# Centring and splitting the last stage's gate and up weights in the grouped attention instead of in the last stage

## The chip, the cores and the metric

The kernel runs on one core of a Trainium2 chip. The metric is the device time of one execution in microseconds (us); the median of three runs is compared. A measurement of this kernel tells a difference of about 0.3%, some 3 us, from none.

## The reference

The program is a network of four layers on 2048 rows (8 sequences of 256) of width 128 in float32. Each layer is an attention and a feed-forward part, each of the form x = x + layernorm(part(layernorm(x))). The two parts between which the change moves work are these:

```python
# layer 2: grouped attention (16 query heads, 4 groups), then an FFN with one of 8 experts for each sequence
raw = einsum('bsgwe,btge->bstgw', Q, K / 8);  attn = softmax(raw, axis=2)
A = einsum('bstgw,btge->bsgwe', attn, V);     attention = X + A @ Wpost
logits = gelu(last_token @ Wp1 + bp1) @ Wp2 + bp2;  sel = argmax(softmax(logits))
h = gelu(hidden @ W1[sel] + b1[sel]);         ffn = hidden + 0.3 * ((h @ W2[sel] + b2[sel]) @ Wo + bo)
# layer 3 (the last stage): attention over channels, then a mixture of 8 experts, H = 342
z = softmax(einsum('byq,byk->bkq', q, k) / sqrt(128));  attention = merge(einsum('byz,bvy->bvz', z, v)) @ Wo.T
w, sel = top_k(distance(x, centroid), 2);  w = softmax(w)
for e in range(8):
    h = silu(xs @ Wg[e] + bg[e]) * (xs @ W1[e] + b1[e])
    out = out + we[:, e:e+1] * (h @ W2[e] + b2[e])
```

## The kernel before

The rows stay in SBUF for the whole run, and the stages follow each other: attention and experts of layer 0, attention and FFN of layer 1, grouped attention with its FFN (layer 2, some 540 to 842 us), and the last stage (layer 3, 843 us to the end). Each engine has an instruction stream of its own; semaphores order them.

**Split weights.** A float32 product is made from three matmuls of rounded parts. For the last stage, the gate and up weights of an expert are a tile of 128 x 684 (128 rows of the hidden width, 2 x 342 columns). They have to be centred (less their last row, spread over all partitions: the tile `last_row`), then rounded (`gu_hi`), and what the rounding left is the low part (`gu_lo`). The matmuls of the experts read `gu_hi`, `gu_lo` and `down`.

**Who does it before.** At the end of the grouped attention SyncE loads the raw weights of all 8 experts into `gu_lo` ("gu", L1525), the plane of last rows ("plane", L1527) and the down weights ("down", L1530). In the last stage VectorE subtracts the last row (`less_last`, L2244 to L2247), ScalarE copies with rounding (`high`, L2430 to L2432), and VectorE subtracts the rounded part (`split`, L2249 to L2252): 24 operations for 8 experts. `mixed_events` (L1986) lists the order of the last stage's first part by hand: for each of the 4 runs of 512 rows the channel attention (`c_stats`, `c_norm`, `c_proj`, `c_scores`, `c_zn`, `c_shift`, `c_res`), the router (`stats`, `norm`, `score`), and the sending of rows to the experts' blocks by GpSimd (`send`, L1712). VectorE, ScalarE and TensorE run through the same list. The tables `less`, `highs` and `splits` say behind which event each of the 24 operations stands. TensorE waits for all splits (`split_ready`, L2691) ahead of the first expert block.

**The grouped attention.** `grouped_attention_ffn` (L2717) runs a pipeline of steps s = 0 to 12, each with 8 sub-steps u, over 8 sequences: in step s, sequence s - 2 is turned and its row maxima are taken, sequence s - 3 is scored, s - 4 is scaled, s - 5 is normed and added to x. GpSimd adds two halves of the probabilities once for each u (`key_halves`, L2897) and does a few small operations (input and output reciprocal roots, L2907, and the residual). SyncE's loop runs over s = 2 to 12 and has only DMAs: `place(s - 3, 1)`, then `spread(s - 4)`, then `place(s - 2, 0)` (L2819, L2831). `place` brings row maxima into the operand `maxima`, which TensorE needs for the scores (L3369); `spread` sends reciprocals out to DRAM and back. Each waits for semaphores, and SyncE handles them strictly one after another. Behind the loop SyncE waits for the last transposed scores, and then `ffn.load_experts(0)` (L348) loads the experts that the first sequences have chosen: six DMAs, for which it reads the choices (`choose`, VectorE, L397). "gu" follows, then the experts of the other sequences, "plane" and "down". The FFN's `first` matmul (L524) waits for the experts.

Of the kernel before, what the change touches and what calls it, by code (L numbers as in the profile page):

```python
# [9 lines left out]
F32 = mybir.dt.float32  # L10
# [1503 lines left out]
def load_experts(eng, layer, src_gu, src_down, w, plane=None, parts=("gu", "plane", "down")):  # L1514
# [9 lines left out]
    if "gu" in parts:  # L1524
        eng.dma_start(w["gu_lo"][:, :, :].bitcast(F32), src_gu[0:n, :, :].rearrange("e p f -> p e f")).then_inc(w["loaded"], 16)  # L1525
    if plane is not None and "plane" in parts:
        eng.dma_start(w["last_row"][:, :, :], plane.rearrange("p (e f) -> p e f", e=n)).then_inc(w["loaded"], 16)  # L1527
# [6 lines left out]
def expert_weights(nc, ctx, layer):  # L1534
# [10 lines left out]
    else:  # L1545
        w["last_row"] = sb("last_row", [P, n, width], F32)
# [439 lines left out]
def mixed_events(W):  # L1986
# [3 lines left out]
    less = {("c_stats", 0): [0], ("c_stats", 1): [1], ("c_norm", 1): [2], ("c_scores", 0): [3], ("c_stats", 2): [4],  # L1990
            ("stats", 0): [5], ("norm", 1): [6], ("stats", 2): [7]}
    highs = {("c_norm", 0): [0, 1], ("c_zn", 0): [2, 3], ("norm", 0): [4, 5], ("norm", 1): [6], ("norm", 2): [7]}
    splits = {("c_norm", 1): [0, 1], ("c_shift", 0): [2, 3], ("c_shift", 1): [4], ("c_shift", 2): [5], ("norm", 2): [6],
              ("c_shift", 3): [7]}

    def with_weights(e):
        return ([e] + [("high", s) for s in highs.get(e, [])] + [("split", s) for s in splits.get(e, [])]
                + [("less_last", s) for s in less.get(e, [])])

    events = with_weights(("c_stats", 0)) + with_weights(("c_norm", 0))  # L2000
    for k in range(RUNS + 3):
# [6 lines left out]
        for e in step:  # L2008
            if 0 <= e[1] < RUNS and e[0] in ("ranked", "routed"):
                events += ranked if (e[0] == "ranked") == (d == RUNS // 2) else []  # L2010
            elif 0 <= e[1] < RUNS and (e[0] != "early" or d == RUNS // 2):
                events += with_weights(e)
# [7 lines left out]
def experts(nc, g, layer, key, w, mix=None, out=None, route=None, load_next=None):  # L2020
# [17 lines left out]
    with ExitStack() as ctx:  # L2038
# [37 lines left out]
        hi_ready, split_ready = st.sem("hi_ready"), st.sem("split_ready")  # L2076
# [11 lines left out]
        if by_distance:  # L2088
            c2_ready, c2_ps, less_ready, stored = (st.sem(n) for n in ("c2_ready", "c2_ps", "less_ready", "stored"))
# [55 lines left out]
        def _(sp):  # L2145
            if not by_distance:
                load_next(sp)
# [68 lines left out]
        def _(dve):  # L2216
# [26 lines left out]

            def less_last(e):  # L2244
                dve.wait_ge(w["loaded"], w["parts"])
                raw_gu = raw_gate_up(w, layer, e)
# [1581 lines left out]
```

## Time and profile before

| | |
|---|---|
| median of three runs | 1046.18 us (1043.87 to 1046.47) |
| profiled execution, its time | 1044.56 us |
| profiled execution, its span | 1042.8 us |
| TensorE (PE) busy | 929.9 us, 89% of the span |
| VectorE (DVE) busy | 685.3 us, 66% |
| ScalarE (ACT) busy | 518.3 us, 50% |
| GpSimd (POOL) busy | 462.1 us, 44% |

A profile is one execution; busy time counts instructions at work, not waits. The views used below are: stretches (busy time of each engine, TensorE's granted clock, share of the DMA engines), groups by line (mean duration of one instruction, and idle time before them), waits (an engine's instruction, what released it, us in all, times, longest), a single tile's or line's instructions, the page's list of DMA issues, and the timeline (start, duration, line, and in brackets the idle time before with its releaser). SPq is SyncE issuing DMAs. In names, `a_` is the attention's tile, `m_` the mixture's, `e_` an expert weight.

### The profile page before, as it was taken

The numbers are of one execution on the slowest core, as the hardware profiler recorded it, in microseconds if no ns is written. First come the engines' busy times: TensorE is split into PE (matmuls) and PEld (weight loads), VectorE is DVE, ScalarE is ACT, GpSimd is POOL, SyncE is SP. The second block draws the span as 40 slices with busy tenths as digits, with TensorE's granted clock in tenths as the row PEclk, the third lists the DMA queues.
The fourth block names the chain that finished last, engine by engine and source line by source line (L and its number), as shares of the span: only waits on it lengthen the run. The fifth ranks groups of instructions, "written<-read, shape, count | busy, mean of one in ns | idle before, by whom it ended". The sixth has DMA issues, their size and how long they took to land. (4 is left out here: it accounts for less than half of the span.)

```text
span 1042.8 us, 23846 instructions
## 1 busy us (share of the span) xinstructions
PE 929.9 (89%) x8240; PEld 730.2 (70%) x8240; DVE 685.3 (66%) x1910; ACT 518.3 (50%) x1023; POOL 462.1 (44%) x512
## 2 busy tenths in 40 slices
PE   7998989799993899999989999999999977869990
PEld 6666667698993766565776676776766866869990
DVE  4687874565445778888487658676577777764444
ACT  2566654244443378786545545444445434324442
POOL 2355554555445313232463334333456432685443
PEclk9999998999997999999999999999999988989996
DMA  8421100222213024222210011110121820022214
GB/s 276 110 74 56 60 2 2 70 68 68 59 42 87 12 74 140 64 64 66 71 32 2 5 40 43 43 42 3 42 43 42 275 77 1 27 67 72 58 47 121
DMA packets 80750, 66.42 MB, mean 64 GB/s; under 512 B 6706, under 2 KB 73441, under 8 KB 80251
## 3 DMA queue, kind: packets, MB, share of 16 engines
q1 hardware_dynamic: 71899, 54.34, 18.9%
q0 software_dynamic: 4512, 8.47, 2.4%
q10 hardware_dynamic: 4224, 2.10, 0.8%
q8 instruction: 70, 1.15, 0.5%
q14 instruction: 45, 0.37, 0.1%
HBM read 38.76 MB, written 26.58 MB: 63 GB/s over the span
## 5 line engine op out<-in xcount | busy, mean ns | idle before, releaser
L832 DVE TENSOR_REDUCE a_rowmax<-a_banks 128x4 f32<-128x1024 f32 (+1 forms) x112 | 136.8, 1221 | 46.6 <-PE a_banks L1245 19.0
L2897 POOL TENSOR_TENSOR a_both<-a_probs 128x512 f32<-128x512 f32 x64 | 85.7, 1340 | 138.7 <-ACT a_probs L3205 138.6
L1057 ACT ACTIVATE a_probs<-a_banks 128x1024 f32<-128x1024 f32 x112 | 114.8, 1025 | 64.7 <-PE a_banks L1231 48.7
L2182 POOL DMA_INDIRECT acc<-m_result,m_yb x77 | 75.7, 983 | 80.1 <-DVE m_result L2319 40.2
L3205 ACT ACTIVATE a_probs<-a_banks 128x1024 f32<-128x1024 f32 x64 | 65.6, 1025 | 89.7 <-PE a_banks L3376 89.7
L2451 ACT ACTIVATE m_gate<-m_banks 128x352 f32<-128x352 f32 (+1 forms) x93 | 42.8, 460 | 97.8 <-PE m_banks L2612 97.7
L3055 DVE TENSOR_REDUCE a_rowmax<-a_banks 128x4 f32<-128x1024 f32 x64 | 77.8, 1219 | 10.2 <-PE a_banks L3349 10.2
L1712 POOL DMA_INDIRECT rows<-m_yrow,m_idx x64 | 64.8, 1012 | 30.6 <-issue 19.3
L700 POOL TENSOR_SCALAR_AFFINE_SELECT a_probs<-a_probs 128x512 f32<-128x512 f32 (+1 forms) x48 | 37.9, 789 | 76.7 <-ACT a_probs L1057 76.7
L3392 PE MATMUL a_banks<-a_probs,a_V 128*64 128x256 f32 x512 | 69.4, 392 | 0.0
L2304 DVE TENSOR_TENSOR m_h<-m_banks,m_gate 128x342 f32<-128x342 f32 (+1 forms) x55 | 28.5, 517 | 55.5 <-ACT m_gate L2451 43.6
L2638 PE MATMUL m_banks<-e_down,m_hT 128*128 (+2 forms) x462 | 64.9, 277 | 0.0
L1195 PE MATMUL a_banks<-ident 128*128 128x128 f32 x374 | 54.3, 292 | 7.7 <-DMA w_att<-in_att 6.1
L2638 PEld LDWEIGHTS m_banks<-e_down,m_hT 128*128 128x128 f32 (+2 forms) x462 | 58.3, 193 | 0.2 <-issue 0.2
L1273 PE MATMUL a_banks<-a_probs,a_V 128*32 128x256 f32 x720 | 58.0, 394 | 0.0
L2610 PE MATMUL m_banks<-e_gu_hi,m_y_hi 128*128 x154 | 56.3, 366 | 0.4 <-issue 0.4
L1195 PEld LDWEIGHTS a_banks<-ident 128*128 128x128 f32 x374 | 48.3, 202 | 11.1 <-DMA w_att<-in_att 6.1
L1231 PE MATMUL a_banks<-a_QT,a_KT 25*128 25x256 f32 x384 | 48.4, 327 | 6.5 <-DVE a_rowmax L832 4.2
L2611 PE MATMUL m_banks<-e_gu_lo,m_y_hi 128*128 x154 | 49.7, 322 | 0.0
L2612 PE MATMUL m_banks<-e_gu_hi,m_y_lo 128*128 x154 | 49.6, 322 | 0.0
L2301 DVE SCALAR_TENSOR_TENSOR m_h<-m_banks,m_yb,m_gate 128x352 f32<-128x352 f32 x38 | 22.2, 583 | 40.9 <-ACT m_gate L2451 40.9
L1245 PE MATMUL a_banks<-a_KT,a_QT 24*128 24x256 f32 x384 | 48.2, 329 | 0.9 <-ACT a_KT L1069 0.9
(420 smaller groups left out, 2552.2 us busy)
## 6 DMA issues: line engine op xcount, KB each, us to landing
rows<-fill SPq DMA_DIRECT2D x16, 520.0 KB, 4.4
a_factor<-recip_rows SPq DMA_DIRECT2D x28, 256.0 KB, 4.7
rows<-fill SPq DMA_DIRECT2D x15, 455.0 KB, 4.2
m_yb<-rows SPq DMA_DIRECT2D x77, 65.0 KB
a_expert<-in_experts SPq DMA_DIRECT2D x16, 257.5 KB, 2.9
e_gu_lo<-in_gu SPq DMA_DIRECT2D x1, 2736.0 KB
e_last_row<-in_last_rows SPq DMA_DIRECT2D x1, 2736.0 KB
e_gu_lo<-in_gu SPq DMA_DIRECT2D x1, 2464.0 KB, 10.2
```

The source lines that it names most:

```text
L832: nc.vector.reduce_max(o, src, AX).then_inc(rowmax_ready, 1)
L1057: nc.scalar.activation(probs[h][:, k, :, :], ps[:, 4:6, :], ACT.Exp, scale=SCALE).then_inc(exp_done, 1)
L1195: mm(ps[:, bank, 0:P], g.ident[:, :], g.ident[:, :], start=True, stop=True)
L1273: last = mm(o[:, 0:SEQ], v, probs[h][:, b // 2 + (0 if causal else 2 * kt), jj, (b % 2) * SEQ:(b % 2 + 1) * SEQ], start=kt == 0, stop=kt = ...
L1712: self.nc.gpsimd.indirect_dma_start(self.rows.rearrange("n p c -> (n p) c"), bass.IndirectOffsetOnAxis(self.idx[:, c:c + 1], 0), self.yrow ...
L2182: nc.gpsimd.indirect_dma_start(acc.rearrange("k n d -> (k n) d"), bass.IndirectOffsetOnAxis(yb[b % YB][:, P:P + 1].bitcast(U32), 0), resul ...
L2610: mm(o, y_hi[i % 3][:, :], gu_hi[:, s], start=True, stop=False)
L2638: last = mm(ps[:, out_bank(i), 0:P], hT[i % 2][0:r, c, :], part[0:r, c, :], start=c == 0, stop=c == FC - 1)
L2897: nc.gpsimd.tensor_tensor(both[u % 4][:, :, :], p[:, :, 0, :], p[:, :, 1, :], ALU.add).then_inc(both_ready, 1)
L3055: nc.vector.reduce_max(rowmax[i % 2][:, :, j, :, n].rearrange("p t h -> p h t"), ps[:, b:b + 2, :].rearrange("p h (t k) -> p h t k", t=T), ...
L3205: nc.scalar.activation(probs[u % 4][:, :, :, :].rearrange("p h t q -> p h (t q)"), ps[:, 4:6, :], ACT.Exp, scale=SCALE).then_inc(exp_done, 1)
L3392: last = mm(ps[h * D64:(h + 1) * D64, 6, 0:SEQ], V[i % 3][:, kt, j, :], probs[b][:, h, kt, :], start=kt == 0, stop=kt == T - 1)
```

## The change

In steps s = 4 to 11 of the grouped attention, expert e = s - 4 is centred, rounded and split. SyncE loads its raw weights into a new tile `centred` and its last-row plane into a new tile `rounded` (`load_raw`, one step ahead). GpSimd subtracts at u = 0, ScalarE copies with rounding at u = 1, GpSimd subtracts at u = 3. SyncE stores both parts to DRAM scratch (`store_split`). Both SyncE parts stand in the loop between `spread` and `place(s - 2, 0)`. There is one pair of tiles, so `load_raw(e + 1)` waits for the stores of e. Behind the loop "lo" is loaded in the place of "gu", after a wait for all stores; "plane" is gone, and "hi" is loaded at the start of the last stage. The 24 operations of the last stage, their semaphores and their three tables are gone, and TensorE waits for the loads where it waited for the splits.

```diff
--- before.py
+++ after.py
@@ -1521,10 +1521,11 @@
         for c in range(FC):
             r = P if c < FC - 1 else last_rows
             eng.dma_start(w["last_down"][0:r, c, :], src_down[n, c * P:c * P + r, :]).then_inc(w["loaded"], 16)
-    if "gu" in parts:
+    if n < NE:
         eng.dma_start(w["gu_lo"][:, :, :].bitcast(F32), src_gu[0:n, :, :].rearrange("e p f -> p e f")).then_inc(w["loaded"], 16)
-    if plane is not None and "plane" in parts:
-        eng.dma_start(w["last_row"][:, :, :], plane.rearrange("p (e f) -> p e f", e=n)).then_inc(w["loaded"], 16)
+    for k in ("lo", "hi"):
+        if split is not None and k in parts:
+            eng.dma_start(w[f"gu_{k}"][:, :, :].bitcast(F32), split[k].rearrange("e p f -> p e f")).then_inc(w["loaded"], 16)
...
@@ -1543,7 +1544,7 @@
         w |= {"last_gu_hi": sb("last_gu_hi", [P, width]), "last_gu_lo": sb("last_gu_lo", [P, width]),
               "last_down": sb("last_down", [P, FC, P], F32), "raw_gu": sb("raw_gu", [P, width], F32)}
     else:
-        w["last_row"] = sb("last_row", [P, n, width], F32)
...
@@ -1987,17 +1988,7 @@
 
 
 
-    less = {("c_stats", 0): [0], ("c_stats", 1): [1], ("c_norm", 1): [2], ("c_scores", 0): [3], ("c_stats", 2): [4],
-            ("stats", 0): [5], ("norm", 1): [6], ("stats", 2): [7]}
-    highs = {("c_norm", 0): [0, 1], ("c_zn", 0): [2, 3], ("norm", 0): [4, 5], ("norm", 1): [6], ("norm", 2): [7]}
-    splits = {("c_norm", 1): [0, 1], ("c_shift", 0): [2, 3], ("c_shift", 1): [4], ("c_shift", 2): [5], ("norm", 2): [6],
-              ("c_shift", 3): [7]}
-
-    def with_weights(e):
-        return ([e] + [("high", s) for s in highs.get(e, [])] + [("split", s) for s in splits.get(e, [])]
-                + [("less_last", s) for s in less.get(e, [])])
-
-    events = with_weights(("c_stats", 0)) + with_weights(("c_norm", 0))
+    events = [("c_stats", 0), ("c_norm", 0)]
     for k in range(RUNS + 3):
         a, b, c, d = k, k - 1, k - 2, k - 3
         step = [("c_shift", c), ("c_res", c), ("c_scores", b), ("c_proj", a), ("stats", c), ("send", d - 1, 3),
@@ -2009,7 +2000,7 @@
             if 0 <= e[1] < RUNS and e[0] in ("ranked", "routed"):
                 events += ranked if (e[0] == "ranked") == (d == RUNS // 2) else []
             elif 0 <= e[1] < RUNS and (e[0] != "early" or d == RUNS // 2):
-                events += with_weights(e)
+                events.append(e)
...
@@ -2143,7 +2133,9 @@
 
         @block.sync
         def _(sp):
-            if not by_distance:
+            if by_distance:
+                load_first(sp)
+            else:
                 load_next(sp)
...
-
-            def less_last(e):
-                dve.wait_ge(w["loaded"], w["parts"])
-                raw_gu = raw_gate_up(w, layer, e)
-                nc.vector.tensor_tensor(raw_gu, raw_gu, w["last_row"][:, e, :], ALU.subtract).then_inc(less_ready, 1)
-
-            def split(e):
-                dve.wait_ge(hi_ready, e + 1)
-                gu_hi, gu_lo, _ = weights(e)
-                nc.vector.tensor_tensor(gu_lo, raw_gate_up(w, layer, e), gu_hi.bitcast(F32), ALU.subtract).then_inc(split_ready, 1)
...
 
         @block.scalar
         def _(act):
-            def high(e):
-                act.wait_ge(less_ready, e + 1)
-                nc.scalar.activation(weights(e)[0], raw_gate_up(w, layer, e), ACT.Copy).then_inc(hi_ready, 1)
...
                 if kind == "slot":
@@ -2688,7 +2660,7 @@
                         pe.wait_ge(route.spot_ready, RUNS)
                     if r == first_early - 1:
                         if by_distance:
-                            pe.wait_ge(split_ready, NE)
+                            pe.wait_ge(w["loaded"], w["parts"])
...
@@ -2755,6 +2727,9 @@
         recip = st.sb("recip", [P, SEQ])
         factor = st.sb("factor", [P, NG, 2, SEQ])
         head_rows = st.sb("head_rows", [P, PAIRS, P])
+        width = 2 * F_EXP[3]
+        centred = st.sb("centred", [P, width], F32R)
+        rounded = st.sb("rounded", [P, width], F32R)
...
@@ -2840,20 +2817,37 @@
                     sp.dma_start(factor[D64 * h:D64 * h + D64, :, n, :],
                                  recip_rows[i % 2, k:k + 1, :, :].to_broadcast([D64, NG, SEQ])).then_inc(factor_ready, 16)
 
+            def load_raw(e):
+                if not 0 <= e < NE:
+                    return
+                if e >= 1:
+                    sp.wait_ge(split_stored, 32 * e)
+                sp.dma_start(centred[:, :].bitcast(F32), raw_gu[e, :, :]).then_inc(raw_loaded, 16)
+                sp.dma_start(rounded[:, :].bitcast(F32), raw_last[:, e * width:(e + 1) * width]).then_inc(raw_loaded, 16)
+
+            def store_split(e):
+                if not 0 <= e < NE:
+                    return
+                sp.wait_ge(low_ready, e + 1)
+                sp.dma_start(split["lo"][e, :, :], centred[:, :].bitcast(F32)).then_inc(split_stored, 16)
+                sp.dma_start(split["hi"][e, :, :], rounded[:, :].bitcast(F32)).then_inc(split_stored, 16)
+
             sp.dma_start(head_rows[:, :, :], head_rows_dram).then_inc(head_rows_loaded, 16)
             for s in range(2, SLOTS):
                 if s - 3 in valid:
                     place(s - 3, 1)
                 if s - 4 in valid and s - 4 != LAST:
                     spread(s - 4)
+                store_split(s - 4)
+                load_raw(s - 3)
                 if s - 2 in valid:
                     place(s - 2, 0)
             sp.wait_ge(sT_ps, S * SEQS)
             ffn.load_experts(sp, 0, experts_dram)
-            last_loads(sp, "gu")
+            sp.wait_ge(split_stored, 32 * NE)
+            last_loads(sp, "lo")
             ffn.load_experts(sp, 1, experts_dram)
             ffn.load_experts(sp, 2, experts_dram)
-            last_loads(sp, "plane")
             last_loads(sp, "down")
 
...
 
+            def less_last(e):
+                pool.wait_ge(raw_loaded, 32 * (e + 1))
+                nc.gpsimd.tensor_tensor(centred[:, :].bitcast(F32), centred[:, :].bitcast(F32), rounded[:, :].bitcast(F32),
+                                        ALU.subtract).then_inc(less_ready, 1)
+
+            def low_part(e):
+                pool.wait_ge(rounded_ready, e + 1)
+                nc.gpsimd.tensor_tensor(centred[:, :], centred[:, :].bitcast(F32), rounded[:, :].bitcast(F32),
+                                        ALU.subtract).then_inc(low_ready, 1)
+
             def key_halves(i, u):
 
                 n = S * i + u
@@ -2900,6 +2904,10 @@
                 i0, i4 = s, s - 5
                 if s - 3 in valid:
                     key_halves(s - 3, u)
+                if u == 0 and 0 <= s - 4 < NE:
+                    less_last(s - 4)
+                if u == 3 and 0 <= s - 4 < NE:
+                    low_part(s - 4)
                 if u == 1 and i0 in valid:
                     in_power(i0)
                 if u == 2 and i4 in valid:
@@ -3276,6 +3284,9 @@
                 i, v = (i2, u - 1) if u else (i2 - 1, S - 1)
                 if i in valid:
                     to_sbuf(i, v)
+                if u == 1 and 0 <= s - 4 < NE:
+                    act.wait_ge(less_ready, s - 3)
+                    nc.scalar.activation(rounded[:, :], centred[:, :].bitcast(F32), ACT.Copy).then_inc(rounded_ready, 1)
...
 
+        split = {k: nc.dram_tensor(f"split_{k}", [NE, P, 2 * F_EXP[3]], F32).ap() for k in ("lo", "hi")}
+
         def load_last(sp, part):
-            load_experts(sp, 3, a["gu3"], a["down3"], w3, a["last_rows"], [part])
-
-        grouped_attention_ffn(nc, g, "att2", a["head_rows"], w3, load_last, "ffn2", a["experts2"])
-        experts(nc, g, 3, "moe3", w3, mix="att3", out=out_dram)
+            load_experts(sp, 3, a["gu3"], a["down3"], w3, split, [part])
+
+        grouped_attention_ffn(nc, g, "att2", a["head_rows"], w3, load_last, "ffn2", a["experts2"], a["gu3"], a["last_rows"], split)
+        experts(nc, g, 3, "moe3", w3, mix="att3", out=out_dram, load_first=lambda sp: load_last(sp, "hi"))
 
```

## Rows read from the trace of the kernel before

**Rows 1.** By stretch: us, busy (count) per engine, TensorE clock, DMA share, GB/s.

```profile
674.00:706.00 32.00, 32.00 (x304) 22.71 (x304) 23.00 (x35) 15.46 (x24) 12.32 (x11) 1.00 0.16 35
...
800.00:843.00 43.00, 38.90 (x262) 33.60 (x260) 32.56 (x127) 16.00 (x36) 22.63 (x31) 1.00 0.64 210
...
843.00:880.00 37.00, 29.87 (x149) 24.91 (x150) 27.97 (x126) 16.36 (x34) 9.31 (x12) 0.82 0.02 5
...
916.00:918.00 2.00, 1.99 (x18) 1.99 (x19) 1.40 (x9) 0.21 (x1) 1.64 (x2) 0.55 0.10 33
```

**Rows 2.** By line, VectorE, 843 to 935 us: busy us, mean ns, idle.

```profile
L2247 DVE TENSOR_TENSOR e_gu_lo<-e_gu_lo,e_last_row 128x684 f32<-128x684 f32 x8 | 6.9, 864 | 1.4 <-DMA e_down<-in_down 1.4
...
L2252 DVE TENSOR_TENSOR e_gu_lo<-e_gu_lo,e_gu_hi 128x684 fp32r<-128x684 f32 x8 | 6.7, 862 | 0.0
```

**Rows 3.** Waits, 843 to 935 us: who, for whom, us, times, longest.

```profile
DVE x L2382 <- ACT m_cf L2438: 3.6, 4, 0.9
...
DVE m_yrow L1757 <- POOL m_in_rstd L1692: 3.5, 3, 1.7
```

**Rows 4.** A tile's and a line's instructions: ns least/median/most, first and last start.

```profile
L2432 ACT ACTIVATE e_gu_hi<-e_gu_lo x8: 760/764/772, 848.1 to 905.8; 128x684 fp32r<-128x684 f32 x8
...
L708 POOL TENSOR_TENSOR e_gu_lo<-e_gu_lo,e_gu_hi x14: 920/924/930, 57.8 to 173.2; 128x352 fp32r<-128x352 f32 x14
...
L1525 SPq DMA_DIRECT2D e_gu_lo<-in_gu x2: 426/430/435, 11.3 to 813.7; - x2
...
L2897 POOL TENSOR_TENSOR a_both<-a_probs x64: 1262/1278/1692, 558.1 to 801.0; 128x512 f32<-128x512 f32 x64
```

**Rows 5.** Page, part 6: DMA issues, KB each, median us to landing.

```profile
a_factor<-recip_rows SPq DMA_DIRECT2D x28, 256.0 KB, 4.7
...
a_expert<-in_experts SPq DMA_DIRECT2D x16, 257.5 KB, 2.9
```

**Rows 6.** Timeline, four engines, 806 to 815 us: start us, us, line, idle before.

```profile
806.20 0.15 DVE L397 FIND_INDEX8 a_chosen<-a_best,a_logits 6x8 uint32<-6x8 f32 x1
...
807.37 6.32 SPq L348 DMA_DIRECT2D a_expert<-in_experts  x6
...
812.57 0.71 POOL L2907 TENSOR_TENSOR a_out_rstd<-a_out_var,minus_half 128x2 f32<-128x2 f32 x1 [5.42 <-DVE a_out_var L2963]
...
814.33 1.89 PE L524 MATMUL a_banks<-a_yT_f,a_expert 128*128 128x256 f32 x8
```

**Rows 7.** Timeline, TensorE, 906 to 921 us, around an idle time.

```profile
906.69 5.60 PE L2533 MATMUL m_banks<-ident 128*128 128x128 f32 x48
...
916.01 0.20 PE L1960 MATMUL m_banks<-m_one_hot,m_upper 128*128 128x64 bf16 x1 [3.72 <-DVE m_chosen L1818]
...
916.31 4.49 PE L2533 MATMUL m_banks<-ident 128*128 128x128 f32 x24
```

**Rows 8.** Timeline, steps 7 to 8 and 9 to 10, two engines.

```profile
700.95 1.35 POOL L2897 TENSOR_TENSOR a_both<-a_probs 128x512 f32<-128x512 f32 x1 [2.00 <-ACT a_probs L3205]
...
715.93 0.43 PE L3369 MATMUL a_banks<-a_maxima,a_ones_row 64*128 64x512 f32 x2
...
763.52 1.29 POOL L2897 TENSOR_TENSOR a_both<-a_probs 128x512 f32<-128x512 f32 x1 [1.00 <-ACT a_probs L3205]
...
774.88 0.50 PE L3369 MATMUL a_banks<-a_maxima,a_ones_row 64*128 64x512 f32 x2 [0.20 <-ACT a_probs L3205]
```

**Rows 9.** Timeline, VectorE and GpSimd, 868 to 931 us.

```profile
868.87 1.56 POOL L1692 TENSOR_TENSOR m_in_rstd<-m_in_var,minus_half 128x4 f32<-128x4 f32 x1 [6.07 <-DVE m_in_var L1750]
...
884.57 1.04 POOL L1692 TENSOR_TENSOR m_in_rstd<-m_in_var,minus_half 128x4 f32<-128x4 f32 x1 [3.69 <-DVE m_in_var L1750]
...
893.71 0.86 DVE L2252 TENSOR_TENSOR e_gu_lo<-e_gu_lo,e_gu_hi 128x684 fp32r<-128x684 f32 x1
...
893.79 1.70 POOL L1712 DMA_INDIRECT rows<-m_yrow,m_idx  x1 [0.19 <-issue]
...
930.20 0.96 POOL L1712 DMA_INDIRECT rows<-m_yrow,m_idx  x1 [0.30 <-issue]
```

More of the change, by code:

```diff
@@ L1511, with load_experts @@
 ROWS_DOWN = {0: F_EXP[0], 3: F_EXP[3] + 1}
-def load_experts(eng, layer, src_gu, src_down, w, plane=None, parts=("gu", "plane", "down")):
+def load_experts(eng, layer, src_gu, src_down, w, split=None, parts=("down",)):
     n = ROUTED[layer]
@@ L1545, in expert_weights @@
     else:
-        w["last_row"] = sb("last_row", [P, n, width], F32)
+        sb("scratch", [P, n, width], F32)
     w["offset"], w["bytes"], w["gu_hi_bytes"] = offset, nc.sbuf_base - offset, 4 * n * width
@@ L2017, in mixed_events, with experts @@
     return events + [("map", 0)] + [("slot", s) for s in range(W + 2)]
-def experts(nc, g, layer, key, w, mix=None, out=None, route=None, load_next=None):
+def experts(nc, g, layer, key, w, mix=None, out=None, route=None, load_next=None, load_first=None):
     width = F_EXP[layer]
@@ L2088, in experts @@
         if by_distance:
-            c2_ready, c2_ps, less_ready, stored = (st.sem(n) for n in ("c2_ready", "c2_ps", "less_ready", "stored"))
+            c2_ready, c2_ps, stored = (st.sem(n) for n in ("c2_ready", "c2_ps", "stored"))
             (c_in_var, c_in_rstd, c_y_ready, c_yT_ps, c_yT_ready, c_qk_ps, c_qk_ready, c_v_ps, c_v_ready, c_z_ps,
@@ L2398, in _ @@
                     route.share(dve, r)
-                if kind == "less_last":
-                    less_last(r)
-                if kind == "split":
-                    split(r)
                 if kind == "early":
@@ L2496, in _ @@
                     route.ratio(act, r)
-                if kind == "high":
-                    high(r)
                 if kind == "gap" and r == RUNS - 1 and by_distance:
@@ L2714, with grouped_attention_ffn @@
 GQA = [("wq", NH * D64), ("wk", NG * P), ("wv", NG * D64), ("wpost", NH * D64)]
-def grouped_attention_ffn(nc, g, key, head_rows_dram, w, last_loads, ffn_key, experts_dram):
+def grouped_attention_ffn(nc, g, key, head_rows_dram, w, last_loads, ffn_key, experts_dram, raw_gu, raw_last, split):
     SCALE = float(D64) ** -0.5
@@ L2773, in grouped_attention_ffn @@
         q_raw, k_raw = st.sem("q_raw"), st.sem("k_raw")
+        raw_loaded, less_ready, rounded_ready, low_ready, split_stored = (
+            st.sem(n) for n in ("raw_loaded", "less_ready", "rounded_ready", "low_ready", "split_stored"))
         both_ready, head_rows_loaded, factor_ps = (st.sem(n) for n in ("both_ready", "head_rows_loaded", "factor_ps"))
```

1 line of the change is left out of this document (removed).

## The prediction

> **What bounds the kernel now.** I read the view of stretches first [rows 1]. In a steady step of the grouped attention (674 to 706 us) TensorE is busy for all of its 32.00 us at full clock, while VectorE has 23.00, ScalarE 15.46 and GpSimd 12.32: work put on the last two there has cover. Between 800 and 843 us, where the selected feed-forward (FFN) runs, TensorE is again nearly full (38.90 of 43). In the first part of the last stage, 843 to 880 us, nobody is: TensorE 29.87 of 37 at a mean clock of 0.82, VectorE 27.97. That is a chain that goes round the engines, and an instruction costs there only what no other engine's delay covers.
>
> So I read next what the change takes out [rows 2]: eight subtractions in L2247, 864 ns each, and eight in L2252, 862 ns: 13.8 us of VectorE. The waits say what stood behind them [rows 3]: four times VectorE reached the residual L2382 and still waited for ScalarE, 3.6 us in all, and three times it waited for GpSimd before L1757, 3.5 us in all. Most of the 13.8 us were put into such gaps.
>
> **The change part by part.**
>
> New work in the attention. A 128x684 subtraction on GpSimd has no row; the nearest are 128x352 at 0.924 and 128x512 at 1.278 us [rows 4], which is 2.2 ns for a column, so I take 1.66 us. Sixteen are 26.5 us on GpSimd, two in each of steps s = 4 to 11, and eight copies of 0.764 us [rows 4] on ScalarE. The first of a step (less_last, u = 0) stands behind the key halves of u = 0, the second (low_part, u = 3) behind those of u = 3. For the steady steps I charge 0: GpSimd is free for over 19 us of a step. Without that cover the pair would cost 3.3 us a step.
>
> The wait on SyncE. store_split stands in the SP loop and waits for low_part. In step s = 11 that is low_part(7), and on GpSimd it is behind the reciprocal root of step 11, u = 2 (L2907), which waits for the attention's sequence 6 and runs at 812.57 for 0.71 us [rows 6]. So low_part(7) ends at 812.57 + 0.71 + 1.66 = 814.9. What is queued behind SyncE's wait are the FFN's six expert loads. They were chosen when L397 ended (806.20 + 0.15 = 806.35), and the first was issued 1.02 us later, at 807.37 [rows 6]. Now SyncE issues two stores at 814.9 (0.43 us each [rows 4] and a small gap, 0.95 in all) and then needs the same 1.02: the first expert load is issued at 816.9. From issue to landing the median is 2.9 us for an expert [rows 5], so it lands at 819.8 at the earliest. It shares the DMA engines with the two stores of 342 KB; the slowest similar row, 4.7 us [rows 5], gives 821.6. I take 820.3, nearer to the expert's own row. TensorE began the first expert's matmuls at 814.33, with no idle time before them [rows 6]. So it starts **6.0 us** later (5.5 to 7.3). Nothing else is queued on TensorE there, and the FFN after it is TensorE's own stretch [rows 1], so the delay goes to the end. The load of "lo" behind the experts moves too, by about 9 us; its need is over 100 us away.
>
> The clock after that gap. After an idle time of 3.72 us (until 916.01) the granted clock was 0.55 in 916 to 918 [rows 1, 7], that is mostly at the lower of the two levels, 1.2 GHz. 24 filler matmuls took 4.49 us there, where 48 of the same kind took 5.60 before [rows 7]: a loss of 4.49 - 2.80 = 1.7 us. The new gap is longer. I take **2 us** (0 to 3.3: nothing if the loads set the pace in those microseconds anyway, twice the row's if the low level lasts twice as long).
>
> The step from s = 9 to s = 10. SyncE's place(7, 0) puts row maxima where the scores of u = 0 of step 10 read them. TensorE used them at 774.88 [rows 8]. Now store_split(5) and load_raw(6) stand before it. low_part(5) follows the key halves of 763.52 + 1.29 = 764.8 [rows 8] and ends at 766.5; two stores are issued by 767.4; their landing has no row, and I bound it by 2.9 and 4.7 us [rows 5]: 770.3 to 772.1; two raw loads are issued in 0.95; then the first two place transfers, about 0.6 us each, and their own landing, for which I have no row but the 2.9 us of an expert [rows 5]: 775.4 to 777.2 in all. The stall is 0.5 to 2.3 us, 0 if so small a transfer lands sooner, 3 if the raw loads hold it up. I take **1.5 us**. In a steady step the key halves of u = 3 start at 700.95 and the next step's scores at 715.93 [rows 8]: 15.0 us, where step 9 has 11.4. The same sum leaves 1.3 to 3.1 us to spare there: 0, bounded at 1 for each of five steps.
>
> The last stage. Taken out are the sixteen VectorE and eight ScalarE operations, and the wait for all weights ahead of the first. Gone through one after the other along the timeline, I find these gains. First, the wait for the weights falls away, at most its 1.4 us idle [rows 2]; but TensorE, which was at 0.82 of its clock in 843 to 880 [rows 1], bounds the steps behind it, and I take 0.4. Second, GpSimd's root L1692 takes 1.56 us when a removed subtraction runs beside it, 1.04 when none does [rows 9]: 0.5 us, and VectorE waits for that one. Third, from 890 to 922 us GpSimd's row sends bound the chain, and a send that meets a removed subtraction (893.71) takes 1.70 us instead of 0.96 [rows 9]; two more are alike (1.59 at 898.83, 1.69 at 911.03). Three times about 0.7 are 2.1, of which the filler matmuls ahead of the ranks let perhaps 1.2 through. The other thirteen subtractions lie under the waits of rows 3 or under TensorE, and come to 0. Sum: a gain of **2 us** (0.4 if only the first counts; 5 if half-clock stretches vanish as well). The cover is ScalarE's cf and GpSimd's sends; they are late next.
>
> On the third gain the Trainium skill's page "SBUF — State Buffer", section "Who interferes with whom", says otherwise: a VectorE tensor_tensor takes only the read interface that it shares with GpSimd and should not hold up descriptor generation. The rows differ (1.70 beside one, 0.96 without), so I go by them. By that page the gain would be about 0.9 instead of 2.
>
> TensorE's new wait for the weights costs 0: "hi" is issued as the last stage begins, and the first block's matmuls come over 80 us later.
>
> Sum: 6.0 + 2 + 1.5 - 2 = +7.5 us. The profiled execution took 1044.56 us, 1042.8 of it span; so that would be 1052.1. The median of the three runs is 1.6 higher, 1046.18; against it the forecast is **1053.7 us**.
>
> **The rivals.**
>
> Faster. VectorE is the engine that bounds the last stage and the freed time is worth its length: the sixteen subtractions give 13.8 us, the attention and FFN cost 9.5: -4.3, 1041.9. For it speaks that VectorE is busy for three quarters of 843 to 880. Against it speak the waits of rows 3 and that fillers and GpSimd's sends set most of the steps. It decides from a gain above 12.6 us in the last stage.
>
> No change. The expert loads don't come late, because the hold on SyncE is shorter than I read or something else of the FFN hides it: 1.5 - 2 = -0.5, 1045.7. Only the order of the code speaks against it, but strictly: one queue, one wait.
>
> Slower still. Every one of the steps 4 to 9 stalls for its row maxima, not the last alone: five more at about 1.5 us, 1061. For it speaks that SyncE's new chain of store, landing, load is some 8 us long in each step; against it the 1.3 to 3.1 us to spare.
>
> **How the numbers follow.** A measurement of this kernel tells 0.3% from no change, 3.1 us. The forecast's mechanism has 0.72, and its own range is 1048 to 1060: all low ends (5.5 + 0 + 0 - 5) would give 1046.7, all high ones (7.3 + 3.3 + 3 - 0.4) 1059.4. Slower still has 0.07, no change 0.13, faster 0.08. The low end of the forecast reaches below 1049.3, which I count as 0.03. So slower by over 0.3% is 0.76, within it 0.16, faster 0.08. For eight in ten the range has to reach into no change or into slower still: 1046.5 to 1060.
>
> **What would show it.** In the profile after, the six expert loads are issued at about 817 to 823, not 807; TensorE idles some 6 us before the first expert's matmuls, with a low clock behind it; SyncE's wait before is for GpSimd's low_part. GpSimd's subtraction is near 1.66 us. The scores of s = 10 wait for the transfer of row maxima. In the last stage the sends at 890 to 922 are all near 1 us, and the first block comes 2 us sooner after the stage's begin. I would be wrong if the expert loads are issued before 812, or if the last stage is shorter by more than 5 us.

## The result and the profile after

Over 20 runs of each kernel the median went from 1044.21 to 1048.86 us. The ratio is 1.0037 with a 95% interval of 1.002 to 1.0054: 3.9 us slower (2.1 to 5.6), where +7.5 was forecast; the two medians alone are 4.7 us apart, inside that interval. The sign and the place were right; the size came out at about half.

The profiled execution of the changed kernel took 1046.88 us. The first lines of its page, the span and the busy time of each engine:

```profile
span 1045.2 us, 23878 instructions
...
PE 923.8 (88%) x8240; PEld 725.4 (69%) x8240; DVE 675.2 (65%) x1894; ACT 518.1 (50%) x1023; POOL 483.7 (46%) x528
```

VectorE lost 10 us of busy time and GpSimd gained 22; TensorE was busy for 6 us less and yet the span is 2.4 longer. The stretches that answer to [rows 1]:

```profile
674.00:706.00 32.00, 32.00 (x302) 22.46 (x300) 22.30 (x35) 16.49 (x26) 15.97 (x13) 1.00 0.28 76
...
800.00:843.00 43.00, 35.86 (x225) 31.27 (x218) 28.16 (x118) 14.89 (x33) 20.75 (x27) 0.96 0.52 164
843.00:880.00 37.00, 28.95 (x161) 23.38 (x159) 20.07 (x102) 11.60 (x25) 9.03 (x15) 0.86 0.22 77
```

A steady step of the attention still has TensorE full for 32.00 us, with GpSimd at 15.97 instead of 12.32: the two subtractions are hidden there, as predicted. In 800 to 843 us TensorE lost 3 us and some clock. SyncE's timeline shows why, and GpSimd's the instruction it waited for:

```profile
812.24 0.33 SPq L2832 DMA_DIRECT2D split_lo<-a_centred  x1
812.61 0.43 SPq L2833 DMA_DIRECT2D split_hi<-a_rounded  x1
814.49 5.90 SPq L348 DMA_DIRECT2D a_expert<-in_experts  x6
820.43 0.43 SPq L1528 DMA_DIRECT2D e_gu_lo<-split_lo  x1
```

```profile
809.90 0.71 POOL L2915 TENSOR_TENSOR a_out_rstd<-a_out_var,minus_half 128x2 f32<-128x2 f32 x1 [5.44 <-DVE a_out_var L2971]
810.59 1.63 POOL L2891 TENSOR_TENSOR a_centred<-a_centred,a_rounded 128x684 fp32r<-128x684 f32 x1
```

The choice of experts was ready at 803.53 + 0.15 = 803.7 here. The loads could have been issued 1 us after that, at 804.7. They were issued at 814.49, behind the last low part (it ends at 812.22) and its two stores. TensorE's timeline, with the idle time and its releaser in brackets:

```profile
806.30 5.52 PE L3517 MATMUL a_banks<-late_w_att,a_craw 128*128 128x128 f32 x48
817.74 3.34 PE L524 MATMUL a_banks<-a_yT_f,a_expert 128*128 128x256 f32 x8 [5.92 <-DMA a_expert<-in_experts]
```

The first expert's matmuls waited 5.92 us for their weights and then took 3.34 us where [rows 6] has 1.89.

**Two single profiles have to be laid on a common event.** The attention's first matmul stands at 538.62 us before and at 532.71 after, though nothing ahead of it was changed: 5.9 us of chance. From there to the end the changed kernel took 8.3 us longer (2.4 + 5.9). Of these, 1.5 lie ahead of the attention's first key halves (21.0 us after its first matmul, where the kernel before has 19.45). They aren't the change's: e2 and h1, which run the attention of the kernel before, have 21.15 there. The following table therefore counts from event to event, read from the timelines of all the profiles of this study, one profile for each kernel: (a) first to last key halves of the attention, against the kernel before; (b) last key halves to the first expert's matmul; (c) from there to the last stage's first matmul; (d) to its first expert block; (e) to the end.

| kernel | a | b | c | d | e |
|---|---|---|---|---|---|
| before | 0 | 13.4 | 30.1 | 86.0 | 112.4 |
| after | +1.7 | 19.5 | 31.2 | 84.0 | 112.3 |
| e1, last store behind the loads | +1.4 | 13.4 | 32.2 | 81.9 | 111.5 |
| e2, last stage alone | 0.0 | 13.4 | 30.1 | 82.0 | 112.2 |
| e3, attention alone | +1.3 | 19.3 | 31.6 | 87.3 | 113.7 |
| e4, store and place moved | +2.3 | 13.4 | 32.0 | 81.8 | 112.1 |
| f1, SyncE's order rewritten | +2.3 | 13.4 | 30.5 | 83.9 | 111.4 |
| f2, all a step or more earlier | +1.0 | 13.4 | 30.1 | 81.8 | 111.5 |
| g3, after with fillers in the gap | +1.0 | 19.9 | 30.2 | 83.8 | 111.9 |
| h1, before with fillers | +0.2 | 13.4 | 30.1 | 86.0 | 114.5 |
| g1, before with three small subtractions | +0.2 | 13.4 | 30.1 | 88.2 | 112.1 |
| g2, before with three one-input operations | +0.2 | 13.4 | 30.1 | 88.1 | 112.0 |

Some 1.4 us in column a of e4 and f1 come from a stretch at the lower clock in step 3 that the other kernels don't show; whether their order brings it about stays open.

### The profile page after: what moved, and what is told of

Read it like the earlier page. It is cut to its first block and busy times, and to the rows that moved or that the text cites. A ratio compares the mean times of both kernels' runs of the same rounds, so it can differ in the third digit from the quotient of the medians.

```text
span 1045.2 us, 23878 instructions
## 1 busy us (share of the span) xinstructions
PE 923.8 (88%) x8240; PEld 725.4 (69%) x8240; DVE 675.2 (65%) x1894; ACT 518.1 (50%) x1023; POOL 483.7 (46%) x528
## 3 DMA queue, kind: packets, MB, share of 16 engines
q8 instruction: 70, 1.15, 0.5%
## 5 line engine op out<-in xcount | busy, mean ns | idle before, releaser
L1713 POOL DMA_INDIRECT rows<-m_yrow,m_idx x64 | 62.2, 972 | 32.5 <-issue 19.9
L1195 PEld LDWEIGHTS a_banks<-ident 128*128 128x128 f32 x374 | 47.0, 198 | 12.4 <-DMA w_att<-in_att 6.7
L2595 PE MATMUL m_banks<-ident,m_h 128*128 128x128 f32 (+2 forms) x279 | 47.0, 277 | 2.1 <-issue 0.7
```

The lines of the kernel that those rows point to most:

```text
L1195: mm(ps[:, bank, 0:P], g.ident[:, :], g.ident[:, :], start=True, stop=True)
L1713: self.nc.gpsimd.indirect_dma_start(self.rows.rearrange("n p c -> (n p) c"), bass.IndirectOffsetOnAxis(self.idx[:, c:c + 1], 0), self.yrow ...
```

## Experiments

**e1: the last store behind the expert loads.** My theory A was the sum of the prediction; theory B, that the last stage gives back about 5 us and not 2.

```diff
-                store_split(s - 4)
+                if s - 4 != LAST:
+                    store_split(s - 4)
...
             ffn.load_experts(sp, 0, experts_dram)
+            store_split(LAST)
             sp.wait_ge(split_stored, 32 * NE)
```

> The changed kernel with one thing moved: SyncE stores the last expert's parts (e = 7) behind the first FFN expert loads, not ahead of them. Theory A (my sum: the late expert loads cost 6.1 us and the low clock behind them 1.5, the attention costs 1.7, the last stage gives back 2.2): the expert loads are issued about 1 us behind the choice, TensorE has no idle time before the first expert's matmuls, and the time is that of the kernel before -0.5 us (-2 to +1). Theory B (the last stage gives back about 5 us on average, and the two single profiles compared hide that): the same repair of the loads, and the kernel before -3.5 us. Theory C (the FFN makes up for late loads, and the changed kernel's cost lies in the attention): the kernel before +3 us, as in the changed kernel.

Measured: 0.9985 of the kernel before (0.9955 to 1.0014), 1.6 us faster with an interval from 4.7 faster to 1.5 slower, which holds A and B and leaves out C. Column b is back at 13.4 us, so one DMA pair in SyncE's queue made the whole delay. Column c is 2.2 us longer than before instead, which none of the theories had. SyncE and TensorE of this run:

```profile
819.48 0.33 SPq L2832 DMA_DIRECT2D split_lo<-a_centred  x1
...
824.04 0.37 SPq L1528 DMA_DIRECT2D e_gu_lo<-split_lo  x1
830.04 2.20 SPq L348 DMA_DIRECT2D a_expert<-in_experts  x2
```

```profile
836.06 1.10 PE L524 MATMUL a_banks<-a_yT_f,a_expert 128*128 128x256 f32 x4 [2.16 <-DMA a_expert<-in_experts]
```

The 2.7 MB of "lo", issued at 824.04, go ahead of the other sequences' experts, issued at 830.04, and TensorE waits 2.16 us for these. In the kernel before, the load of the same size was issued 0.6 us ahead of the first expert's matmul, here 5.2 us behind it. The Trainium skill's page "DMA: Bandwidth & Descriptors", section "Queues, rings and completion order", has each ring consumed in order on its DMA engine; these rows agree, and f1 below tests it.

**e2: the last stage's part alone.** The attention is that of the kernel before, the 24 operations are left out, and raw weights are loaded where the parts would be:

```diff
-        split = {k: nc.dram_tensor(f"split_{k}", ...).ap() for k in ("lo", "hi")}
+        split = {"lo": a["gu3"].rearrange("e p f -> p e f"), "hi": a["last_rows"].rearrange("p (e f) -> p e f", e=NE)}
```

> The last stage's part of the change alone: the grouped attention is that of the kernel before, the 24 operations of the last stage are left out, and raw weights of the same size are loaded where the finished parts would be (so centring and splitting are left out of the computation). Theory A: the kernel before -2.2 us (-1 to -3.5). Theory B: the kernel before -5 us. If VectorE bound the last stage: -10 us or more.

Measured: 0.995 (0.992 to 0.998), 5.2 us faster (2.1 to 8.4): nearest to theory B, though the interval's end touches the 2.2 of theory A (f2 below decides). Laid on the kernel before at the last stage's first matmul, the first block comes 4.0 us sooner, and the timelines show where. 0.27 us: the wait for the weights (2.0 us gained at first, of which TensorE's own chain takes back the rest). 0.55: the root of [rows 9] takes 1.01 us instead of 1.56. 1.15: a stretch at the lower clock is gone (below). What is left, 2.07, goes nearly all to three sends, together 1.88 us shorter. Two of them on GpSimd's timeline; the first answers to the send of 1.70 us in [rows 9], the second took 1.59 before:

```profile
892.70 1.03 POOL L1713 DMA_INDIRECT rows<-m_yrow,m_idx  x1 [0.19 <-issue]
...
896.89 1.03 POOL L1713 DMA_INDIRECT rows<-m_yrow,m_idx  x1 [0.20 <-issue]
```

Each shortening reaches the next send. Between the second and the third stand filler matmuls and the ranks: ahead of them the sends come 3.46 us sooner than in the kernel before, behind them 3.32, so the fillers take only 0.14. The first block gets the rest.

For the clock, TensorE's timeline of the kernel before at one matmul (channel values of the second 512 rows), then the stretch of 12 us from 24 us into the stage; a stretch's row ends with the granted clock, the DMA share and GB/s:

```profile
870.21 1.13 PE L2571 MATMUL m_banks<-m_parts,m_czn 128*128 128x256 f32 x4 [2.36 <-DVE m_czn L2279]
```

```profile
868.40:880.40 12.00, 9.89 (x51) 9.39 (x52) 9.40 (x55) 5.47 (x11) 4.76 (x4) 0.72 0.01 1
```

The same two views of e2:

```profile
870.13 1.13 PE L2543 MATMUL m_banks<-m_parts,m_czn 128*128 128x256 f32 x4 [1.58 <-DVE m_czn L2261]
```

```profile
869.40:881.40 12.00, 9.58 (x62) 8.00 (x62) 8.80 (x53) 4.71 (x10) 4.70 (x4) 1.00 0.00 1
```

With the removed subtractions TensorE idled 2.36 us ahead of that matmul and then was granted 0.72, so over half of the 12 us at the lower of the two levels, 1.2 GHz; without them it idled 1.58 us and kept 2.4 GHz. All seven profiles with the new last stage have 1.00 in that stretch; of the five with the old one only h1 has.

**e3: the attention's part alone.** The attention of the changed kernel, then "gu", "plane" and the last stage of the kernel before:

```diff
             sp.wait_ge(split_stored, 32 * NE)
-            last_loads(sp, "lo")
+            last_loads(sp, "gu")
...
+            last_loads(sp, "plane")
             last_loads(sp, "down")
```

> The attention's part of the change alone: all loads, the 24 operations and the stores to scratch in the grouped attention with SyncE's waits as in the changed kernel, while the last stage is that of the kernel before with raw weights and its own 24 operations. Theories A and B: the kernel before +9.3 us (7.5 to 11). Theory C: the kernel before +3 to +5 us.

Measured: 1.0096 (1.0072 to 1.0119), 10.0 us slower (7.5 to 12.4). The prediction's terms for the attention, 6.0 + 2 + 1.5, make 9.5. TensorE's first expert matmul in this run:

```profile
821.47 3.74 PE L524 MATMUL a_banks<-a_yT_f,a_expert 128*128 128x256 f32 x8 [5.79 <-DMA a_expert<-in_experts]
```

With e2 the two halves add up: 10.0 - 5.2 = 4.8 us, against 3.9 (2.1 to 5.6) for the whole change.

**e4: store and place moved.** As e1, with the row maxima placed between the store and the next raw load.

```diff
+                if s - 2 in valid:
+                    place(s - 2, 0)
                 load_raw(s - 3)
-                if s - 2 in valid:
-                    place(s - 2, 0)
```

> As the run with the last store behind the expert loads, and in SyncE's loop the row maxima of the next sequence are placed between the store of the finished parts and the load of the next raw weights. Theory A: the stall of 1 us between steps 9 and 10 is gone too, and the time is the kernel before -1.7 us (-3 to 0). Theory B: the kernel before -4.5 us. If placing the maxima first holds up the raw loads, GpSimd's subtraction at u = 0 starts later and the key halves behind it wait: then it is slower than the run with the last store moved alone.

Measured: 0.9968 (0.9952 to 0.9984), 3.3 us faster (1.7 to 5.0), between A's 1.7 and B's 4.5. Past the 1.4 us in step 3, the second to fourth key halves of step 10 are late by 0.3 us, where e1's are late by 0.7 and the changed kernel's by 1.0. So putting the row maxima behind the raw loads cost 0.4 to 0.7 us in these two profiles. It varies from profile to profile: e3, with the attention of the changed kernel, has 0.8 there, and g3, whose attention is that of the changed kernel line for line, only 0.4, that is 0.1 above e4. GpSimd's own work makes the rest.

**f1: SyncE's order rewritten.** Theory D is theory B with what e1 and e4 showed. As e4, with the first raw load ahead of the loop and "lo" behind the experts of all sequences.

```diff
             ffn.load_experts(sp, 0, experts_dram)
+            store_split(LAST)
-            sp.wait_ge(split_stored, 32 * NE)
-            last_loads(sp, "lo")
             ffn.load_experts(sp, 1, experts_dram)
             ffn.load_experts(sp, 2, experts_dram)
+            sp.wait_ge(split_stored, 32 * NE)
+            last_loads(sp, "lo")
```

> The changed kernel with SyncE's order rewritten: the first raw weights are loaded before the loop; in the loop the row maxima are placed between the store and the next raw load; the last store stands behind the first expert loads, and the parts lo behind the other sequences' expert loads too. Theory D (the attention then costs only 0.7 us for GpSimd's work in step 10; TensorE waited 2.16 us for the other sequences' experts in the run with the last store moved, because the 2.7 MB of lo went ahead of them, and that goes; the last stage gives back 4 to 5): the kernel before -3.5 to -4.5 us, no DMA wait of TensorE in the FFN. Rival (lo collides with something else when it comes later, or the last stage gives back only 2): the kernel before -1.5 us or more.

Measured: 1.0012 (0.9986 to 1.0039). TensorE's DMA wait in the FFN is gone (column c: 30.5, where e1 and e4 have 32.2 and 32.0), as expected. The total is not: 1.3 us slower than before, with an interval from 1.5 faster to 4.1 slower, which leaves out what D expected and lies where the rival has it. (The medians of these runs, 1044.45 and 1045.03, have it 0.6 us faster.) Neither of the rival's reasons shows in the profile: TensorE doesn't wait for "lo", and column d has 83.9, 2.1 less than before. Its profile shows 1.4 us at the lower clock in step 3 and one more stretch (0.80 and 0.93 granted, 36 to 50 us into the last stage); it doesn't show the rest, so this total stays unexplained.

**g1 and g2: the sends.** In the kernel before, three subtractions beside sends (split of e = 5 and 7, centring of e = 7) are cut to 2 columns (g1), or replaced by one-input operations on the same 684 columns (g2).

```diff
-                nc.vector.tensor_tensor(gu_lo, raw_gate_up(w, layer, e), gu_hi.bitcast(F32), ALU.subtract).then_inc(split_ready, 1)
+                n = 2 if e in (5, 7) else 2 * F_EXP[layer]
+                nc.vector.tensor_tensor(gu_lo[:, 0:n], raw_gate_up(w, layer, e)[:, 0:n], gu_hi.bitcast(F32)[:, 0:n], ALU.subtract).then_inc(split_ready, 1)
```

```diff
+                if e in (5, 7):
+                    nc.vector.tensor_scalar(gu_lo, raw_gate_up(w, layer, e), 0.5, 0.25, ALU.subtract, ALU.mult).then_inc(split_ready, 1)
```

The first is g1's split, the second g2's; the centring of e = 7 is changed alike.

> The kernel before, with three of the last stage's subtractions cut to 2 of their 684 columns: those beside which a row send took 1.6 to 1.7 us (the split of e = 5 and 7, the centring of e = 7; so three experts' parts are not computed). By my prediction three sends get 0.6 to 0.7 us shorter and 1.2 us of that reach the first block. Theory D: the sends get shorter and all of it, about 2.0 us, reaches the first expert block, counted from the last stage's first matmul (in the kernel before 86.0 us). If the sends' length has nothing to do with the subtractions: 86.0.

> The kernel before, with the same three subtractions replaced by operations on one input of the same 684 columns (subtract and multiply by constants; so three experts' parts are not computed). If it is the second SBUF input that holds up a send beside it: sends of about 1.0 us there, and the first block 1.5 to 2 us sooner than 86.0. If any long VectorE instruction does: sends stay longer than 1.3 us there.

In g1 the three sends take 1.04, 1.04 and 1.03 us instead of 1.70, 1.59 and 1.69. Set against the kernel before, the sends behind them come 0.66, 0.56 and 0.65 us sooner than those ahead of them: 1.87 of 1.87 us reach the next send. The first block doesn't come sooner, though: 88.2 us where 84.0 was expected. The granted clock is 0.64 and 0.72 in 42 to 50 and 50 to 58 us. TensorE, behind with its fillers, takes up the rows that the ranks need 2.4 us after they are ready, and the sends lose 2.3 us there, more than the first two shortenings. Such a fall from 42 to 50 us is in e3 too (0.79), whose last stage is that of the kernel before; the one from 50 to 58 is in g1 and g2 alone, and whether their edits bring it about stays open. So g1 shows what the subtractions do to the sends; that the gain reaches the first block, e2 alone shows. In g2 the three sends take 1.03, 1.03 and 1.33 us, the first of them beside this:

```profile
896.51 0.51 DVE L2256 TENSOR_SCALAR e_gu_lo<-e_gu_lo 128x684 fp32r<-128x684 f32 x1
```

A one-input operation of the same width takes 0.51 us instead of 0.86 and leaves this send at its normal length; the third send, beside another, is in between. The second one comes too late for its send and meets the one behind it, which keeps its 0.96 us, only in its last 0.2 us:

```profile
900.64 1.03 POOL L1712 DMA_INDIRECT rows<-m_yrow,m_idx  x1 [0.20 <-issue]
901.98 0.96 POOL L1712 DMA_INDIRECT rows<-m_yrow,m_idx  x1 [0.30 <-issue]
```

```profile
902.72 0.54 DVE L2248 TENSOR_SCALAR e_gu_lo<-e_gu_lo 128x684 f32<-128x684 f32 x1
```

In the kernel before, each of the three subtractions begins 0.08 to 0.18 us ahead of its send ([rows 9] has 893.71 and 893.79). In g2 only the third operation does (914.50 and 914.59), and its send is the one of 1.33 us; the first begins 0.2 us after its send. The one-input operation is also the shorter one. So g2 doesn't separate the second input from the length or from which of the two begins first. The Trainium skill's page "SBUF — State Buffer", section "Who interferes with whom", lets a two-input tensor_tensor take only a read interface shared with GpSimd and infers from this that it should not hold up descriptor generation. Here the measurement decides: 1.59 to 1.70 us beside one, 1.03 without.

**h1: fillers in the last stage of the kernel before.**

```diff
-                keep_busy((0, 4, 4, 0)[r], 5)
+                keep_busy((0, 13, 4, 0)[r], 5)
```

> The kernel before with 9 more filler matmuls of 128 columns in TensorE's idle time of 2.36 us ahead of the channel values of the second run of 512 rows (22 to 26 us into the last stage). If it is this idle time that brings the clock down in the 7 us after it (granted 0.66 in 870 to 880), the clock stays at its higher level there and the first rank matmul comes about 1.1 us sooner than 43.1 us after the stage's first matmul. If the clock falls there by its own time, nothing changes, or the fillers delay what they stand before.

TensorE's timeline at the place, and the stretch that had 0.72 before:

```profile
867.21 3.06 PE L2533 MATMUL m_banks<-ident 128*128 128x128 f32 x26
870.62 1.13 PE L2571 MATMUL m_banks<-m_parts,m_czn 128*128 128x256 f32 x4 [0.35 <-DVE m_czn L2279]
```

```profile
868.80:880.80 12.00, 10.19 (x71) 8.76 (x70) 9.85 (x57) 6.34 (x12) 5.25 (x4) 1.00 0.00 0
```

The clock stays up there, and the first rank matmul comes at 41.9 us instead of 43.1, as expected. But it falls later (0.89 in 894.8 to 910.8), behind the idle time ahead of the same matmul of the next 512 rows, and the first block is at 86.0 us as before. That idle time is just as long in the kernel before, and there the matmul runs at the higher clock. First h1, then the kernel before:

```profile
900.25 1.90 PE L2571 MATMUL m_banks<-m_parts,m_czn 128*128 128x256 f32 x4 [1.93 <-issue]
```

```profile
901.08 1.10 PE L2571 MATMUL m_banks<-m_parts,m_czn 128*128 128x256 f32 x4 [1.93 <-issue]
```

So the idle time of 2.36 us brings the first fall about, and filling it alone moves the fall to a later idle time. The length of an idle time alone doesn't say whether a fall follows. h1, like g1 and g2, is a single execution.

**g3: fillers in the gap of the changed kernel.**

```diff
             pe.wait_ge(craw_ready, PAIRS * SEQS)
+            busy(24, 6)
             ffn.first(pe, 0)
```

> The changed kernel with 24 filler matmuls (5.5 us at the higher clock) on TensorE in the idle 5.9 us in which it waits for the late FFN experts; they write a bank that the first expert's matmul overwrites. Prediction's step: the gap costs 1.5 us more by the low clock behind it. If so, the first eight matmuls of the expert take 1.9 us and not 3.3, and from the first expert's matmul to the last stage's first takes 30.1 us and not 31.2; the whole is 1.1 to 1.5 us faster than the changed kernel, so the kernel before +2.5 us (0 to +5, as the clock falls elsewhere). Rival: the expert's loads set the pace there, and nothing changes.

```profile
814.41 5.52 PE L3336 MATMUL a_banks<-ident 128*128 128x128 f32 x48
820.89 2.04 PE L524 MATMUL a_banks<-a_yT_f,a_expert 128*128 128x256 f32 x8 [0.96 <-DMA a_expert<-in_experts]
```

The first matmuls take 2.04 us instead of 3.34 and column c is 30.2 instead of 31.2: the clock's price behind the gap is 1.0 us. The total, 1.0037 (1.0024 to 1.005), can't tell 1 us from nothing.

**f2: all of it earlier.** Two experts in the long step 3, then one in each step to step 9, the stores behind the placing, "lo" behind all expert loads:

```diff
+LESS = {(3, 0): 0, (3, 5): 1} | {(e + 2, 2): e for e in range(2, NE)}
+ROUND = {(3, 1): 0, (3, 6): 1} | {(e + 2, 3): e for e in range(2, NE)}
+LOW = {(3, 2): 0, (3, 7): 1} | {(e + 2, 4): e for e in range(2, NE)}
...
+                if s == 3:
+                    store_split(0)
+                    load_raw(1)
                 if s - 2 in valid:
                     place(s - 2, 0)
+                if s >= 3:
+                    store_split(s - 2)
+                    load_raw(s - 1)
```

> The changed kernel with all eight experts centred and split in steps 3 to 9 (two of them in the long step 3, then one in each step: subtraction at u = 2, copy at u = 3, subtraction at u = 4), the stores behind the placing of the next row maxima, and the parts lo loaded behind all expert loads. So GpSimd has none of it in steps 10 and 11, and SyncE waits for none of it near the FFN. Theory D: the attention costs nothing (key halves of step 10 within 0.3 us of the kernel before, counted from the first ones), no late expert loads, and the last stage gives back 2 to 4 us depending on where the clock falls: the kernel before -2 to -4 us. Rival (what the new loads and stores cost in the attention is traffic, not order): the key halves of step 10 come 1 us later as before, and the whole is the kernel before -1 us or no change.

Measured: 0.9953 (0.9937 to 0.9968), 4.9 us faster than before (3.3 to 6.6) and so faster than both kernels; D expected 2 to 4. SyncE near the FFN:

```profile
790.48 3.19 SPq L2820 DMA_DIRECT2D a_factor<-recip_rows  x4
810.95 19.86 SPq L348 DMA_DIRECT2D a_expert<-in_experts  x8
830.86 0.44 SPq L1528 DMA_DIRECT2D e_gu_lo<-split_lo  x1
```

No store stands there, and the first load is issued 1.0 us after the choice (809.78 + 0.15), as in [rows 6]. Columns b and c are those of the kernel before. The attention is 1.0 us longer, not free as expected: 0.7 of it arise in step 9, where all the work now ends, so in that part the rival was right.

## Why the prediction was off, step by step

**Right: the late expert loads.** Counted on the timeline of the kernel before (L397 ended 2.67 us sooner in the profile after), the first load was issued at 817.2 and the first matmul began at 820.4; the steps said 816.9 and 820.3. Column b grew by 6.1 us for a predicted 6.0. e1 shows that it is SyncE's order alone.

**Right in kind: the clock behind the gap.** 2 us were taken, 1.0 to 1.5 measured (g3 and column c), inside the bounds.

**Right in sum, wrong in its parts: steps 9 to 11.** 1.5 us for the row maxima; measured 1.7 in column a. TensorE did wait for them, and for less than predicted:

```profile
769.49 1.08 PE L3403 MATMUL a_banks<-a_probs,a_V 128*64 128x256 f32 x8
771.56 0.50 PE L3380 MATMUL a_banks<-a_maxima,a_ones_row 64*128 64x512 f32 x2 [0.98 <-DMA a_maxima<-a_mrow]
```

This wait is 0.64 us in e1, 0.70 in e3 and 0.32 in g3, which keep the row maxima behind the raw loads; in the kernel before, e4, f1 and f2 the same matmul waits 0.20 us, for ScalarE. The 3 us that the prediction named as the other possibility didn't come. Column a of the four kernels with that order has 1.7, 1.4, 1.3 and 1.0. The rest arises in step 10 from its low part on; f2, which has no GpSimd subtraction in that step, adds only 0.2 there. That the low part holds up the FFN's own GpSimd work is argued, not tested. The charge of 0 for the steady steps held to 0.03 us in each, but step 10 isn't one. GpSimd's subtractions, by line, with their mean in ns, were estimated at 1.66 us:

```profile
L2886 POOL TENSOR_TENSOR a_centred<-a_centred,a_rounded 128x684 f32<-128x684 f32 x8 | 13.5, 1692 | 0.0
L2891 POOL TENSOR_TENSOR a_centred<-a_centred,a_rounded 128x684 fp32r<-128x684 f32 x8 | 13.2, 1646 | 0.0
```

**The step that failed: the last stage's gain, 2 us.** Measured 5.2 alone (e2). In column d the seven profiles with the new stage average 82.7 us and the two of before and e3 86.6: 3.9 us; column e adds 1.2, for which no cause was tested. f2 rules out 2 us without any profile: it is 3.3 to 6.6 us faster, and its attention gives nothing back. With 5.1 in place of 2 the sum is 6.1 + 1.1 + 1.7 - 5.1 = 3.8, the measured 3.9. That it fits so closely is luck, since the 1.7 is one profile's; with the mean of the four kernels, 1.4, the sum is 3.5. Two terms of the gain were mis-sized. Of the sends' 2.1 us I let 1.2 through, "the filler matmuls ahead of the ranks" taking the rest; e2 shows that the fillers took 0.14 us, since GpSimd's queue of sends is itself the chain there. They take more where the clock is low, as in g1. And the clock, which the prediction named only as the end of its range ("5 if half-clock stretches vanish as well"), does belong in it: the stretch at 0.72 was brought about by an idle time that the removed work made longer. The wait for the weights (0.4 predicted, 0.3) and the root (0.5, 0.55) were right. So was the reading that most of the 13.8 us of VectorE lay in waits, as the waits after show, against [rows 3]:

```profile
DVE x L2364 <- ACT m_cf L2412: 7.4, 4, 2.5
...
DVE m_yrow L1758 <- POOL m_in_rstd L1693: 2.6, 3, 1.1
```

VectorE now waits 7.4 us for ScalarE's cf where it waited 3.6: the work went, and the wait took its place.

**The rivals.** "Faster" needed 12.6 us from the last stage; it gives 5. "Slower still" needed stalls in every step; steps 4 to 8 show none. "No change" rested on the loads coming in time, and they didn't. That the profile after shows a first block exactly 2.0 us sooner (84.0) looked like a confirmation; it is the slowest of the seven. Column d of these takes two values: 83.8 to 84.0 in the changed kernel, f1 and g3, where the granted clock is 0.76 to 0.88 from 36 to 50 us into the stage, and 81.8 to 82.0 in the other four, where it is 1.00. So one profile could give a gain of 2 or of 4, as the clock fell.

## What to carry to other kernels

Work that is hidden on its own engine can still cost at the in-order queue that stores its result: here a 1.63 us subtraction, itself behind a root that waited 5.44 us, had six loads issued 9.8 us later than they could be. With the work done up to two steps earlier and the stores and "lo" moved back in SyncE's queue, 3.9 us lost became 4.9 gained. When work is taken out of a stage where no engine is full, don't count its own time: count what it stretched on the serial chain beside it, and the idle times it made longer on TensorE, with the clock behind them. And lay two profiles on a common event ahead of the change before subtracting them.

## What the hardware showed that was not expected

- A two-input subtraction of 128x684 on VectorE lengthens a GpSimd row send beside it from 1.03 to between 1.59 and 1.70 us, and a root of 128x4 from 1.01 to 1.56. Beside a one-input operation of the same width (0.51 us) one send took 1.03 and one, which began after the operation, 1.33.
- An idle time of 2.36 us was followed by 0.72 of the clock over 12 us, one of 1.58 us and one of 0.35 us at the same place by 1.00. Where the first was filled, the clock fell behind a later one of 1.93 us, which another kernel passed at 1.00.
- Code that wasn't changed ended 5.9 us apart in two profiled executions, more than the change itself.
